# Transposed scores kept in PSUM for three of four attentions, stablemax as two terms added by TensorE, router logits on TensorE

## The reference

```
x = x + tanh(g_xattn[0]) * xattn0(layernorm(x), ctx)      # 16 heads of 64
x = x + tanh(g_ffn[0])   * moe0(layernorm(x))             # 8 experts, top 1, capacity
x = x + tanh(g_xattn[1]) * xattn1(layernorm(x), ctx)      # softmax
x = x + tanh(g_ffn[1])   * bitlinear(layernorm(x))
x = x + tanh(g_xattn[2]) * xattn2(layernorm(x), ctx, mask)# masked softmax, heads mixed before Wo
x = x + tanh(g_ffn[2])   * moe2(layernorm(x))             # 8 experts, top 2
x = x + tanh(g_xattn[3]) * xattn3(layernorm(x), ctx)      # stablemax
x = x + tanh(g_ffn[3])   * moe3(layernorm(x))             # 8 experts, top 1, capacity

score = einsum('bhqd,bhkd->bhqk', q, k) / sqrt(8)
out   = einsum('bhqk,bhkd->bhqd', softmax(score), v)      # then @ Wo + bo
stablemax: s = where(x >= 0, x + 1, 1 / (1 - x));  s / sum(s)
```

## Time and profile before

| | us |
|---|---|
| time, median of 3 runs | 3624.97 (3622.75 to 3628.83) |
| time of the profiled execution | 3616.34 |
| its span | 3614.6 |
| attention 2, 968.6 to 1427.3 | 458.7 |
| attention 3, 1725.4 to 2411.5 | 686.1 |
| attention 4, 2680.3 to 3387.0 | 706.7 |

### The profile page before, as it was taken

One profiled execution on the slowest core, in us unless ns is written; L12 is line 12 of the kernel. 1 busy time (PEld: TensorE's weight loads), 2 busy tenths in 40 slices (PEclk: granted clock), 3 DMA queues, 4 the chain that ended last, 5 costly groups with the idle time before them and its releaser, 6 DMA issues. The chain is left out here.

```text
span 3614.6 us, 84054 instructions
## 1 busy us (share of the span) xinstructions
PE 2554.5 (71%) x30961; PEld 1981.4 (55%) x30971; DVE 2132.0 (59%) x4394; ACT 1498.5 (41%) x2492; POOL 1596.1 (44%) x2184
## 2 busy tenths in 40 slices
PE   5999999977678886233687766609956877665490
PEld 4878778764557775122465555506634665554260
DVE  3767777661166664676578788854424666677312
ACT  3555555532255553677343333202215665553120
POOL 1333433440164430775024666440017788884207
PEclk9999999988888887555688778659976766675795
DMA  4000000003300000000000000015531000000243
GB/s 143 17 18 22 23 21 21 20 8 112 99 26 22 22 19 13 1 1 1 26 10 12 23 22 23 20 61 153 161 106 32 23 25 27 27 23 13 79 128 93
DMA packets 192979, 153.50 MB, mean 42 GB/s; under 512 B 24426, under 2 KB 170461, under 8 KB 192582
## 3 DMA queue, kind: packets, MB, share of 16 engines
q1 hardware_dynamic: 176198, 116.45, 11.0%
q0 software_dynamic: 16384, 31.69, 2.9%
HBM read 97.54 MB, written 52.43 MB: 41 GB/s over the span
## 5 line engine op out<-in xcount | busy, mean ns | idle before, releaser
L979 PE MATMUL l_B<-l_val,l_prob_t 128*64 128x18 f32 x6144 | 348.6, 220 | 44.1 <-ACT l_prob_t L822 36.9
L979 PEld LDWEIGHTS l_B<-l_val,l_prob_t 128*64 128x64 f32 x6144 | 340.4, 149 | 59.3 <-issue 59.3
L903 PE MATMUL l_PT<-const_table,l_prob 128*128 128x128 f32 x1536 | 267.9, 332 | 38.0 <-ACT l_prob_t L822 28.6
L1971 PE MATMUL experts_H<-experts_xs_t,experts_w 128*128 128x512 f32 x576 | 272.1, 616 | 10.1 <-ACT experts_hid L1951 4.9
L903 PEld LDWEIGHTS l_PT<-const_table,l_prob 128*128 128x128 f32 x1536 | 237.3, 178 | 68.8 <-issue 58.0
L822 ACT COPY l_prob_t<-l_PT 128x512 f32<-128x512 f32 x384 | 209.6, 601 | 132.8 <-PE l_PT L903 132.7
L203 POOL DMA_INDIRECT l_got<-rows,l_index x192 | 220.2, 1147 | 94.7 <-POOL l_index L196 50.3
L358 POOL TENSOR_TENSOR l_products<-l_router_w,xn_all 128x1024 f32<-128x1024 f32 x100 | 236.3, 2390 | 32.3 <-DVE logits L464 32.0
L883 PE MATMUL l_A<-const_table,l_xn 128*128 128x128 f32 x192 | 59.6, 410 | 251.7 <-issue 139.1
L328 POOL DMA_INDIRECT slots<-xn_all,put x192 | 202.0, 1052 | 60.6 <-issue 49.5
L632 POOL TENSOR_TENSOR l_var_eps<-l_mv,eps 128x2 f32<-128x2 f32 x96 | 26.4, 275 | 430.4 <-DVE l_mv L775 430.3
(11 more groups left out here) (309 smaller groups left out, 6835.8 us busy)
## 6 DMA issues: line engine op xcount, KB each, us to landing
experts_w<-in_F_w SPq DMA_DIRECT2D x104, 256.0 KB, 2.9
experts_xs<-slots SPq DMA_DIRECT2D x72, 256.0 KB, 2.8
rows<-experts_y SPq DMA_DIRECT2D x72, 256.0 KB, 2.9
l_ctx_t<-in_ctx_t SPq DMA_DIRECT2D x96, 128.0 KB, 2.1
slots<-l_zeros SPq DMA_DIRECT2D x64, 96.0 KB
experts_w<-in_F_w SPq DMA_DIRECT2D x40, 128.0 KB, 2.5
slots<-l_zeros SPq DMA_DIRECT2D x8, 512.0 KB, 5.5
l_ctx_t<-in_ctx_t SPq DMA_DIRECT2D x64, 64.0 KB, 2.0
```

The lines of the kernel that those rows point to most:

```text
L903: last = nc.tensor.transpose(PT[:, c % 2, P * a:P * a + P], prob[:, t.par(5), c, a // 2, 2 * (a % 2):2 * (a % 2) + 2, :].rearrange("p j k ...
L979: last = nc.tensor.matmul(B[64 * b:64 * b + 64, col:col + 18], prob_t[:, 4 * (hp // 2) + 2 * tile + hp % 2, 64 * b:64 * b + 64], val[:, t. ...
L1971: nc.tensor.matmul(H[:, c, :], w1_s[:, t.par(2), c, :], xs_t[:, t.par(2), :], start=True, stop=True).then_inc(h_filled[c], 1)
```

## The change

`attention_narrow` and `Tail` are gone. A new function `attention_split` takes their place for attentions 2 to 4, with the class `Router` of the wide attention (changed so that normalised rows go to their final place at once, without POOL's copy).

- Scores for the probabilities are made transposed, keys on partitions (PE, `Z`), so that they need no transposing afterwards. In the two softmax attentions the scores are made a second time with queries on partitions (`X`) for the maximum alone; VectorE takes it from PSUM, splits it into three bfloat16 parts, TensorE transposes them, VectorE spreads them over a diagonal (`top_d`, 128 x 1024), and TensorE subtracts them in PSUM by a matmul with -1. ScalarE takes Exp from PSUM straight to `prob_t`, in 4 instructions of 512 columns.
- The mask of attention 3 is added in PSUM, by matmuls of the identity with `hide` (bfloat16), for both kinds of scores.
- Stablemax keeps its two terms apart: VectorE's max(x, 0) and ScalarE's exp(-ln(1 + max(-x, 0))) are each multiplied with V, and TensorE adds the products.
- The zeros around a head's rows stay in `q_m` and `k_m` from the start of the stage. ScalarE writes q and k once each (`q_t`, `k_t`), and SP copies them, 8 partitions at a time, from SBUF to SBUF.
- V is multiplied with the heads by 64 matmuls of 64 rows, 64 columns and 9 moving columns (128 of them with stablemax), where there were 32 of 128 rows and 18 moving columns.
- The biases of V and of the output are added as bfloat16 rows in three parts.
- Router logits: TensorE transposes the normalised rows and multiplies them with the router's weights.
- POOL's gathering takes its indices where they are, without a copy first, and comes behind the combining in a beat.

The core of the diff, with lines left out:

```diff
-                if t.live(2):
-                    wait(sp, v_filled, done_v)
-                    sp.dma_start(ctx_t[:, t.par(2), :], g.ctx_t[:, bass.ds(t.item(2) * 256, 256)]).then_inc(
...
+            def step(t):
+                if t.live(2):
+
+                    wait(sp, xv_filled, beats(t.t - 2, TURN, XV_BEATS) if t.t >= 8 else 0)
+                    sp.dma_start(ctx_t[:, t.par(2, 6), :], g.ctx_t[:, t.item(2) * 256:t.item(2) * 256 + 256]).then_inc(ctx_in[t.par(2, 6)], 16)
+                if t.live(PROJ):
+                    slot = t.par(PROJ, 3)
+                    if not stable:
+
+                        wait(sp, qk_drained, t.done(PROJ))
+                        wait(sp, s_filled, t.done(PROJ + 3))
+                        for row in range(0, P, 8):
+                            sp.dma_start(k_m[row:row + 8, slot, row // 8 % 4, :], k_t[row:row + 8, slot, :]).then_inc(k_masked[slot], 16)
+
+                    wait(sp, qk_drained, t.done(PROJ))
+                    wait(sp, p_filled, t.done(PROJ + 3))
+                    for row in range(0, P, 8):
+                        sp.dma_start(q_m[row:row + 8, slot, row // 8 % 4, :], q_t[row:row + 8, slot, :]).then_inc(q_masked[slot], 16)
...
+                if t.live(PROB) and stable:
+                    for r in range(4):
+
+                        dve.wait_ge(ready, 1)
+                        wait(dve, relu_done, 4 * t.done(PROB) - 3 + r)
+                        wait(dve, o_filled, t.done(PROB + 2))
+                        V.tensor_scalar(prob_t[:, t.par(PROB), r, :], Z[:, r, :], 0.0, None, ALU.max).then_inc(plus_done, 1)
...
+                if t.live(OUT):
+
+                    pe.wait_ge(ready, 1)
+                    wait(pe, prob_done, n7 if stable else 4 * n7)
+                    if stable:
+                        wait(pe, plus_done, 4 * n7)
+                    wait(pe, xv_drained, beats(t.t - 1, TURN, XV_BEATS))
+                    bank_read(t, 2)
+                    bank_read(t, 3)
+                    wait(pe, o_drained, n8)
+                    terms = (prob_t, soft) if stable else (prob_t,)
+                    for h in range(16):
+                        for tile in range(2):
+                            for b in range(2):
+                                rows, side = slice(64 * b, 64 * b + 64), 64 * (b ^ tile)
+                                for k, term in enumerate(terms):
+                                    col = 256 * tile + 64 * (h % 4)
+                                    last = nc.tensor.matmul(Z[side:side + 64, 2 + b, 9 * h:9 * h + 9], term[rows, t.par(OUT), h // 4, col:col + 64],
+                                                            val[rows, t.par(OUT), tile, h, :],
+                                                            start=k == 0, stop=k == len(terms) - 1)
```

More of the change, by code:

```diff
@@ L220, in combine @@
-        if self.own:
-            last = nc.gpsimd.tensor_tensor(self.term[:, 1, :, :], g.xn[:, tiles, :],
-                                           g.weight[1][:, tiles].unsqueeze(2).broadcast_to([P, 2, D]), ALU.mult)
+        wait(pool, self.arrived[par], t.landed(s, 2 * self.ks))
+        wait(pool, self.combined, t.done(s + 1))
+        for k in range(2):
+            last = nc.gpsimd.tensor_tensor(self.term[:, k, :, :], others[k], g.weight[k][:, tiles].unsqueeze(2).broadcast_to([P, 2, D]),
+                                           ALU.mult)
@@ L400, in dve, with transpose @@
-    def dve(self, nc, dve, t, s, updated):
+        return nc.tensor.matmul(bank[:, 0:n], ones, self.before[:, :].unsqueeze(1).broadcast_to([P, BATCH_TILES, EXPERTS]),
+                         start=False, stop=True)
+    def transpose(self, nc, pe, t, s, out):
+        wait(pe, self.xn_done, t.done(s + 2))
+        for tile in range(self.tiles):
+            last = nc.tensor.transpose(out[:, P * tile:P * tile + P], self.g.xn[:, t.item(s + 2) * self.tiles + tile, :], self.g.const[:, C_IDENT:C_IDENT + P])
+        return last
@@ L519, in chain, with beats, attention_split @@
         return link
-def attention_narrow(nc, g, name, gate_col, wq, bq, wk, bk, wv, bv, wo, bo, kind, mask=None, head=None, tail=None):
-    ITEMS, TPI = TILES // 2, 2
+def beats(t, first, n):
+    return max(0, min(t - first + 1, n))
+def attention_split(nc, g, name, gate_col, wq, bq, wk, bk, wv, bv, wo, bo, kind, mask=None, head=None, router=None):
+    ITEMS = TILES // 2
     SCALE = float(1.0 / np.sqrt(np.float32(8)))
-    folded = kind == "masked"
+    HIDE = float(2.0 ** 100)
+    folded, stable = kind == "masked", kind == "stable"
+    STAT, NORM, TURN, PROJ, SCORE, PROB, OUT, STREAM = range(1, 9)
+    LAST = STREAM + 1
     with ExitStack() as ctx:
@@ L615, in _ @@
+            for t in range(2, ITEMS + PROJ):
                 step(Step(sp, ITEMS, t))
@@ L785, in _ @@
+            for t in range(ITEMS + DEPTH - 1):
+                step(Step(dve, ITEMS, t))
             if tail:
@@ new lines, in step @@
+                if turns(t):
+                    act.wait_ge(ready, 1)
+                    wait(act, turned_filled, beats(t.t, TURNED_FROM, TURNED_BEATS))
+                    if not folded and t.live(OUT):
+                        last = nc.scalar.copy(ctx_out_t[:, t.par(OUT), :], TURNED[:, 0:256])
+                    if tail and t.live(T0 + 2):
+                        last = nc.scalar.copy(tail.xn_t[:, t.par(T0 + 2), :, :], TURNED[:, 256:512].rearrange("p (k n) -> p k n", n=P))
+                    last.then_inc(turned_drained, 1)
@@ L941, in step @@
-                if t.live(5):
-                    transpose_probabilities(2)
-                    transpose_probabilities(3)
-                if t.live(6):
-                    pe.wait_ge(ready, READY)
-                    wait(pe, o_drained, n6)
-                    wait(pe, v_drained, n4)
-                    bank_read((xt_drained, n2), (wo_drained if folded else ot_drained, n7), (counts_read, ranks))
+                                last = nc.tensor.matmul(Z[64 * b:64 * b + 64, r, 256 * tile:256 * tile + 256], k_t[rows, slot, seq],
+                                                        q_m[rows, slot, :, seq], start=stable and tile == 0, stop=tile == 1 and not folded)
@@ new lines, in step @@
+                    if folded:
+                        pe.wait_ge(hidden, 2)
+                        for tile in range(2):
+                            for r in range(4):
+                                last = nc.tensor.matmul(Z[:, r, 256 * tile:256 * tile + 256], g.const_bf[:, C_IDENT:C_IDENT + P],
+                                                        hide[:, 1, 2 * t.item(PROB) + tile, :].unsqueeze(1).broadcast_to([P, 4, 64]),
+                                                        start=False, stop=tile == 1)
```

1064 lines of the change are left out of this document (402 added, 662 removed).

## The result

The changed kernel took 4168.76 us in the median (4166.01 to 4169.38, four runs) where before took 3626.9 (3622.75 to 3630.59) beside it: ratio 1.149, interval 1.147 to 1.151. Forecast were 3556, with 3430 to 3730 around it. It is 15% slower, and the prediction was wrong in sign and size.

The account below looks back on a forecast made before the run. The prediction took attentions 2 to 4 to be set by their beat of handovers, with no engine full. Attention 2 +39, attention 3 -66 and attention 4 -41 gave -68 us: 3556 us forecast, range 3430 to 3730.

Parts of the forecast that it names:

- the pitch c: Time on SP's queue from one DMA issue to the next: taken as 0.42 us, bounds 0.39 and 0.56.
- My reading of the 0.43: SP's whole-partition loads: 0.34 us of their own, the rest waiting for the 128 rows of the DMA before.
- 33c + 0.2: Beat of attentions 2 and 3 in us if SP's 33 copies an item set it, c being their pitch.
- T: Length in us of the beat every item repeats: forecast 14.1, 15.2 and 16.3 in attentions 2, 3 and 4.
- 88 + 35T: Length of attention 3: 88 us plus 35 beats, 620 us at a beat of 15.2, a gain of 66.
- 2211c - 1037: Sum of the three stages' changes in us if SP sets attentions 2 and 3; zero at c = 0.47.
- a gain of 41: Attention 4: stage of 665 us, with a beat of 16.3 against 17.5, so 41 us gained.
- The rival with SP's pitch: SP's copies pace like large DMAs: +91 us at 0.51, +201 at 0.56; chance of a slower kernel by this 0.27.
- the order on ScalarE: Attention 4: ln and exp follow the output copy, next scores are read after them, then products; beat 16.3 us.
- 6.0 stood: Attention 4: 256 records of products with V take 6.0 us, bounded by 5.0 and 14.5.
- other loop through SP: Attention 2: 16 copies of k, landing, scores, products of q and k, ScalarE copies, handovers: 12.5 to 14.4 us.
- TensorE at 15.2: Attention 3: TensorE sets the beat, 12.7 us busy and 2.5 waiting for the maximum.

Follow-up runs that it names:

- e1: Changed kernel with weights of q and k permuted so each copy takes 32 rows, 9 DMAs an item in place of 33 (5 for 17 in attention 4); 3691.7 us, ratio 1.020.
- e2: Changed kernel with as many copies, but 16 rows each in place of 8; output not the reference's; 4166.8 us.
- e5: Changed kernel with its 8-row copies reading the context in device memory in place of q and k in SBUF; 3421.9 us.
- e10: e1 with attention 4's copies reading the context in device memory; output not the reference's; 3420.4 us.
- e4: Changed kernel without POOL's gathering and combining in attention 4, copies and scattering kept; 4000.5 us.
- e9: Changed kernel with only POOL's wait for TensorE's products with V added before its indirect DMAs; 4012.8 us.
- e3: Changed kernel with all copies of q and k left out, scores zero; 3649.4 us.
- e14: The kernel of e6 again, in one batch with e13 and e15; 3460.5 us, ratio 0.955.
- e15: The kernel of e3 again (no copies of q and k), in one batch with e13 and e14; 3663.9 us.
- e13: The kernel of e1 again, unchanged, in one batch with e14 and e15; 3711.3 us.
- e17: The kernel of e1 once more, unchanged, in one batch with e18; 3708.0 us.
- e8: The kernel of e1 again, unchanged, in one batch with e9 and e10; 3421.1 us.
- e6: e1 with POOL starting its gathering and scattering only after TensorE's products with V; 3358.0 us, ratio 0.928.
- e7: e6 with the terms interleaved: four first terms of a head, then its four second terms; 3356.9 us, ratio 0.929.
- e18: e6 with the second term of a head written over the first in PSUM, not added; 3452.0 us.

## Why the prediction was wrong

**The step that failed is the pitch c.** "Lower bound for c: 0.39. Upper bound: 0.56": it is 0.67, and the bounds were drawn from rows of another kind. (The upper one was also misread: 1.12 is how long the pair of loads lasts. From its start to the next load it is 1.17, or 0.58 each.) Every row loads from device memory; the new copies read SBUF, and of those the trace of before had none. I varied what I could see (rows, the size of the DMA ahead) and took the rest for equal. e1 and e2 show that the number of rows changes little when the source is SBUF (0.67 for 8, 0.63 for 16, 0.64 for 32, medians), e5 that with 8 adjacent rows the source halves it, e10 that with 32 rows 4 apart it doesn't. What sets the pitch in general stays open; that it is 0.67 for the copies of this change, and that this is what attentions 2 and 3 pay for, is shown. My reading of the 0.43, 0.34 of its own and the rest for the rows of the DMA ahead, is not refuted for loads from device memory, since e5 has 0.335; it was put to use where it doesn't apply.

**The form of the sum was right.** With 33c + 0.2 = 22.3 attention 2 should take 35 + 32 x 22.3 + 12 = 761; it took 758.6. Attention 3 by 88 + 35T gives 868 and took 833.3, 35 less, since its last beats have no copies to wait for. The formula 2211c - 1037 gives a loss of 444 us at 0.67. The measured 549 is 105 more: -2 from attention 2, -35 from attention 3, and 143 from attention 4, which lost 102 where a gain of 41 stood. The rival with SP's pitch had the mechanism and stopped at 0.56 (+201).

**Attention 4** failed at the allowance that wasn't there: nothing in my sum could stop TensorE in the middle of a block. Without the stops the order on ScalarE that I went by is the right one: T = 17.0 (e4), 16.7 (e9), against 16.3. Of the terms, the products measured 7.1 where 6.0 stood: the 19.5 ns of the earlier trace rows were read from the wide attention, at clock 0.98 (500 to 800), and attention 4 runs them at 0.5, which its 0.64 in the earlier trace rows should have told me. SP was indeed hidden there (e3's T is within 0.8 of the changed kernel's), and POOL, which I had expected nearly full, is busy 338.8 us of 808.4: it did its harm by its DMAs. ScalarE and VectorE do behave as forecast; no wait stands between exp and the next reading in the changed kernel.

**What stops TensorE.** Shown: in the bad batches the long blocks of products are those with many packets of POOL's indirect DMAs in them (e1's attention 3), e14 moves these DMAs and takes the stops out of the products, and SP's copies aren't needed (e3, e15). Shown too: the same overlap makes short stops or none in the good batches (e1, e13, e17 against e8). Before, with the same gathering, was as fast in both (3619 to 3630 and 3617 to 3624); whether that is because it has 64 records of products a beat where there are 256 now, no run tests.

My guess was that TensorE runs out of instructions because their loading waits behind POOL's traffic. The profile's DMA queues have one called "instruction" (q8). In the bad beat of the changed kernel, from 3529 to 3537, and then in e8 over one block, 2869.5 to 2877 (packets, MB, share):

```profile
## 3 DMA queue, kind: packets, MB, share of 16 engines
q0 software_dynamic: 192, 0.39, 17.8%
q1 hardware_dynamic: 191, 0.10, 5.1%
issues: line engine op xcount, KB each, median us to landing
```

```profile
q0 software_dynamic: 160, 0.33, 15.3%
q1 hardware_dynamic: 336, 0.26, 12.0%
q8 instruction: 2, 0.03, 1.7%
```

No instruction packet in 8 us of the bad beat, two in the good one. But the trace speaks against the guess. The whole profile has 348 such packets for 85,558 records of TensorE (matmuls and weight loads together), and before 257 for 61,932: 246 and 241 records a packet. The good window has 261 of each, 522 in all, so its two packets are what it used up. In the bad beat one packet came as the stop began, between 3528.5 and 3529.5, and after it TensorE began only 47 of its records until 3537, a fifth of a packet (columns as in the earlier trace rows):

```profile
3529.40:3537.00 7.60, 2.93 (x24) 2.02 (x23) 0.00 (x0) 0.00 (x0) 4.98 (x5) 0.50 0.24 64
```

In two other bad beats (e13, 3044.3 to 3052 and 3069 to 3077) a packet did come during the stop. The missing packets look like what a stop leaves behind, and not like its cause. What POOL's DMAs and TensorE get into each other's way on, and why a batch is of one sort or the other, stays open; where the program lies in memory is one candidate, and no run varied it.

**The rest.** In attention 2 the "other loop through SP" of 12.5 to 14.4 went by 16 copies of k; with 4 of them T is 10.4 (e6), so what was gained on VectorE and ScalarE does pay once SP is out of the way. In attention 3 I had TensorE at 15.2; it is 12.5 as long as nothing is scattered. Both are better than before (12.3 and 17.9): with the copies cut to a quarter and POOL's DMAs moved, the same change is 7% faster than before in a good batch and 4.5% in a bad one.

## What to carry to other kernels

A cost that is multiplied by 33 for each item needs a row of its own kind: the same source, the same destination, the same shape, the same engine. If the trace has none, the bounds should be a factor of two and not a fifth, and the first thing to try is to cut the count: a permutation of the weights made 9 DMAs out of 33 and was worth 464 us. And when a kernel's time differs between batches while its neighbour's doesn't, repeat the base beside the variant before believing the variant.

## What the runs showed of the hardware

- A DMA started by SP that copies rows of 1 KB from SBUF to SBUF takes the queue 0.67 us from one to the next with 8 rows, 0.63 with 16 and 0.64 with 32 (medians; the changed kernel, e2, e8). From device memory it is 0.335 with 8 adjacent rows (e5), but with 32 rows 4 apart it lasts 594 ns, as from SBUF (e10).
- TensorE can stop again and again in a stretch of many short matmuls while POOL's indirect DMAs run: blocks of 256 records took up to 15 us in place of 7.1, in four of the six batches, while the runs of one kernel within a batch agreed to 0.4%. Two batches on the same chip were one of either sort.
- ScalarE, too, stood still for up to 2.8 us a beat in e14, between exp and its next reading of scores.
- A record of the products with V took 15 to 16 ns at clock 1.0 and 27 at 0.5, whatever the order of the terms (e7) and with or without adding in PSUM (e18).
